# Attention's output projection in three passes by token halves, its division on GpSimd, and the next gated layer begun on the first half

## What is computed

```python
def step(carry, inp):                       # linear attention, 16 heads of 128
    state, z = carry
    q_s, k_s, v_s = inp
    ...
    den = jnp.einsum('bhe,bhe->bh', q_s, z)[..., None] + EPS
    return ((state, z), num / den)
...
return out @ Wo.T                           # 2048 -> 256
...
x = x + s * g                               # g = silu(mixture-of-experts layer of xn)
xn = _layernorm(x, axis=-1)
s = _L1_attn_ref(xn, ...)                   # state-space layer, needs xn
g = _silu(_L1_ffn_ref(xn, ...))             # gated layer: down(silu(gate) * up), hidden width 704
x = x + s * g
```

## Time and profile before

| | before |
|---|---|
| median of 3 runs | 1776.23 us (1775.18 to 1776.37) |
| the profiled execution, its own time | 1777.31 us |
| its span (first to last instruction) | 1775.5 us |
| PE busy | 1648.1 us (93% of the span) |
| DVE / ACT / POOL busy | 1156.9 / 760.2 / 664.7 us (65% / 43% / 37%) |
| mean granted clock of TensorE | 0.971 |

### The profile page before, as it was taken

How to read it: one execution, slowest core, us unless ns; L and a number is a source line. 1 busy time by engine, 2 the same in 40 slices (tenths; PEclk the granted TensorE clock), 3 DMA queues, 4 the chain that set the end, 5 groups by cost and what they waited for, 6 DMA issues and landing times.

```text
span 1775.5 us, 29643 instructions
## 1 busy us (share of the span) xinstructions
PE 1648.1 (93%) x11068; PEld 1366.1 (77%) x11068; DVE 1156.9 (65%) x2041; ACT 760.2 (43%) x1393; POOL 664.7 (37%) x500
## 2 busy tenths in 40 slices
PE   5997899898999999999869978998989999999988
PEld 3886677787878888887848857777978888888878
DVE  4333788663767788876743347886536677777767
ACT  4343445433434444444543334553334444444445
POOL 1453444200324444453514534441003244444535
PEclk9998999999999999999979989999999999999999
DMA  2333000000253344341023320000002533443410
GB/s 77 101 108 118 18 37 1 0 1 10 72 166 121 120 137 137 120 134 34 26 68 107 117 94 19 36 1 1 1 10 71 166 120 122 139 134 119 138 29 25
DMA packets 60061, 135.68 MB, mean 76 GB/s; under 512 B 8128, under 2 KB 12736, under 8 KB 59408
## 3 DMA queue, kind: packets, MB, share of 16 engines
q1 hardware_dynamic: 59920, 133.79, 23.6%
HBM read 130.81 MB, written 2.95 MB: 75 GB/s over the span
## 4 chain that ended last, share of the span: by engine, by line
PE 67%; DVE 11%; POOL 7%; issue 6%; ACT 5%; DMA 2%; SPq 0%; POOLq 0%; DVEq 0%; ACTq 0%
PE ps L553 31%; PE ps L610 6%; PE ps L872 4%; PE ps L896 4%; PE ps L649 4%; PE ps L834 3%; PE ps L589 3%; POOL silu_g L451 3%; PE ps L908 3%; POOL rb L469 2%; POOL fw_lo L436 2%; PE ps L883 2%; PE ps L751 2%; PE ps L752 2%; DVE hid L1347 2%
## 5 line engine op out<-in xcount | busy, mean ns | idle before, releaser
L553 PE MATMUL ps<-xnT_hi,w_in_hi 128*128 128x512 f32 x512 | 222.8, 435 | 0.0
L553 PE MATMUL ps<-xnT_lo,w_in_hi 128*128 128x512 f32 x512 | 203.6, 398 | 0.0
L553 PE MATMUL ps<-xnT_hi,w_in_lo 128*128 128x512 f32 x512 | 203.1, 397 | 0.0
L469 POOL TENSOR_TENSOR rb<-ra,rb 128x512 f32<-128x512 f32 x80 | 117.6, 1470 | 205.0 <-DVE rb L1537 205.0
L427 POOL TENSOR_TENSOR w_in_lo<-w_raw,w_in_hi 128x1024 fp32r<-128x1024 f32 x32 | 85.0, 2658 | 224.3 <-ACT w_in_hi L954 224.3
L1347 DVE TENSOR_TENSOR hid<-ps,silu_g 128x512 f32<-128x512 f32 (+1 forms) x80 | 55.1, 689 | 162.4 <-POOL silu_g L451 106.3
L1659 DVE TENSOR_TENSOR_SCAN lmat<-dec,ident 128x512 f32<-128x512 f32 x128 | 160.6, 1295 | 0.0
L516 POOL TENSOR_TENSOR yt<-yg,sz 128x512 f32<-128x512 f32 x64 | 83.5, 1305 | 155.4 <-ACT sz L1265 148.4
L553 PE MATMUL ps<-xnT_hi,fw_hi 128*128 128x512 f32 x312 | 126.7, 406 | 10.5 <-DVE fw_lo L1365 4.3
L436 POOL TENSOR_TENSOR fw_lo<-fw_raw,fw_hi 128x512 fp32r<-128x512 f32 (+1 forms) x56 | 62.7, 1121 | 185.3 <-ACT fw_hi L984 134.6
L1681 DVE TENSOR_TENSOR mt<-ps,lmat 128x512 f32<-128x512 f32 x128 | 82.5, 686 | 66.1 <-PE ps L872 66.1
(11 more groups left out here) (194 smaller groups left out, 4397.8 us busy)
## 6 DMA issues: line engine op xcount, KB each, us to landing
dec<-dec_dram SPq DMA_DIRECT2D x64, 512.0 KB, 4.0
w_raw<-in_w_in SPq DMA_DIRECT2D x32, 512.0 KB, 4.7
wdec<-dec_dram SPq DMA_DIRECT2D x128, 128.0 KB, 3.9
pdec<-dec_dram SPq DMA_DIRECT2D x128, 128.0 KB, 3.7
fw_raw<-in_fw SPq DMA_DIRECT2D x40, 384.0 KB, 3.1
w_raw<-in_w_qkv SPq DMA_DIRECT2D x8, 768.0 KB, 4.2
comb<-comb_dram SPq DMA_DIRECT2D x8, 512.0 KB, 3.7
w_out<-in_w_o SPq DMA_DIRECT2D x2, 2048.0 KB, 10.8
```

Of the source, the lines that this page charges most:

```text
L469: nc.gpsimd.tensor_tensor(rb[:, k], ra[:, k], rb[:, k], ALU.add).then_inc(a_rot.sem, 1)
L553: mm = nc.tensor.matmul(out, left(l, k), right(r, k), start=(j == 0), stop=(j == len(steps) - 1))
```

## The change

**The projection** now goes by token halves and tiles of the inner width: 2 halves x 16 tiles = 32 units `n`. Per unit PE makes 4 transposes (straight from `y`, into bank `n % 3`) and 12 matmuls of 256 columns in three fp32r passes, which gather in banks 4 and 5 for half 0 and 6 and 7 for half 1. `w_out` is split to `wa_hi`, `wa_lo` on the way (in units 0 to 15), and the transposed `y` to `yTs_hi`, `yTs_lo` (3 slots).

**The division** moves from DVE to POOL: 32 instructions per batch of 128 x (4 x 128), in place in `y`. The first six (`EARLY_NORM`) stand ahead of the end of phase 2. DVE only makes `1/den`, in two pairs of small instructions.

**The barrier** behind the projection is gone. The layernorm of chunks 0 to 3 runs in the second half's units, and PE starts `gate_up` (0,0) on the first token half right after the last projection matmul. The gated layer's first four units go in the order (0,0), (1,0), (0,1), (1,1) (`FFN1_ORDER`), and the decay's matmuls go to banks 6 and 7, one half at a time.

The core of the diff (`-` lines of removed helpers that stand in the kernel above are cut):

```diff
+EARLY_NORM = 6
...
+FFN1_ORDER = [(0, 0), (1, 0), (0, 1), (1, 1)] + [(k, hf) for k in range(2, NF1) for hf in range(2)]
...
+                def normalised(n):
+
+                    hf, t = n // NT - 2 * b, n % NT
+                    pool.wait_ge(rin_step, 4 * b + (2 if t < (KVH - 1) * REP else 4))
+                    part = y[:, 4 * hf:4 * hf + 4, t * P:(t + 1) * P]
+                    nc.gpsimd.tensor_tensor(part, part, rin[:, 4 * hf:4 * hf + 4, t:t + 1].broadcast_to([P, 4, P]), ALU.mult).then_inc(o_yn.sem, 1)
+                for n in range(2 * b * NT, 2 * b * NT + EARLY_NORM):
+                    normalised(n)
                 end_phase(pool, b, 2)
-                end_phase(pool, b, 3)
+                for n in range(2 * b * NT + EARLY_NORM, 2 * (b + 1) * NT):
+                    normalised(n)
...
+                def turn(n):
+                    hf, t = n // NT - 2 * b, n % NT
+                    pe.wait_ge(o_yn.sem, o_yn.done(n))
+                    pe.wait_ge(o_yl.sem, o_yl.done(n - 3))
+                    for j in range(4):
+                        mm = nc.tensor.transpose(ps[:, n % 3, j * P:(j + 1) * P], y[:, 4 * hf + j, t * P:(t + 1) * P], ident4[:, 0:P])
+                    mm.then_inc(o_tr.sem, 1)
+
+                def project(n):
+                    hf, t = n // NT - 2 * b, n % NT
+                    if hf == 0:
+                        pe.wait_ge(o_wh.sem, o_wh.done(b * NT + t))
+                        pe.wait_ge(o_wl.sem, o_wl.done(b * NT + t))
+                    pe.wait_ge(o_yh.sem, o_yh.done(n))
+                    pe.wait_ge(o_yl.sem, o_yl.done(n))
+                    for j in range(4):
+                        for x, (l, r) in enumerate(SPLITS):
+                            mm = nc.tensor.matmul(ps[:, 4 + 2 * hf + j // 2, (j % 2) * DM:(j % 2 + 1) * DM], yTs[l][:, n % YSLOTS, j * P:(j + 1) * P],
+                                                  wa[r][:, t, :], start=(t == 0 and x == 0 and j % 2 == 0), stop=(t == NT - 1 and x == 2),
+                                                  skip_group_check=True)
                     mm.then_inc(o_mm.sem, 1)
...
+                turn(n0 + 1)
+                for n in range(n0, n0 + 2 * NT):
+                    if n + 2 < n0 + 2 * NT:
+                        turn(n + 2)
+                    project(n)
+                    t = n - n0 - NT
+                    if t >= 0 and t % 3 == 2 and t // 3 < 4:
+                        ln_transposes((b * 2 + 1) * NC + t // 3, t // 3 % 2, 3)
 
             def out_proj1(b):
 
...
+                def decay(hf):
+
+                    for c in range(2 * (1 - hf), 4):
+                        pe.wait_ge(o_sg.sem, o_sg.done(b * NC + 4 + c))
+                    pe.wait_ge(ln_hi.sem, ln_hi.done((b * 2 + 1) * NC + 4 * hf + 3))
+                    pe.wait_ge(ln_lo.sem, ln_lo.done((b * 2 + 1) * NC + 4 * hf + 3))
+                    return three_passes(ps[:, 6 + hf, :], lambda l, k: w_dec[l][:, k, :],
+                                        lambda r, k: xnT[r][:, k, hf * HALF:(hf + 1) * HALF])
...
+                pe.wait_ge(o_yl.sem, o_yl.done(2 * (b + 1) * NT - 1))
+                pe.wait_ge(ln_hi.sem, ln_hi.done((b * 2 + 1) * NC + 3))
+                pe.wait_ge(ln_lo.sem, ln_lo.done((b * 2 + 1) * NC + 3))
                 gate_up(b, NF0, 0)
-                pe.wait_ge(s_dec.sem, s_dec.done(b))
-                gate_up(b, NF0, 1)
-                for u in range(2 * NF1):
-                    k = (u + 2) // 2
-                    if u + 2 < 2 * NF1:
-                        gate_up(b, NF0 + k, u % 2, together=(k == NF1 - 1))
-                    down(b, NF0 + u // 2, u % 2, u < 2, u >= 2 * NF1 - 2, rows=(64 if u >= 2 * NF1 - 2 else P))
+                ln_turned(4)
+                decay(0)
+                ln_turned(5)
+                gate_up(b, NF0 + 1, 0)
+                ln_turned(6)
+                ln_turned(7)
+                decay(1).then_inc(s_loga.sem, 1)
+                gate_up(b, *ffn1(2))
+                for x in range(2 * NF1):
+                    if 0 < x < 2 * NF1 - 2:
+                        gate_up(b, *ffn1(x + 2), together=(FFN1_ORDER[x + 2][0] == NF1 - 1))
+                    k, hf = FFN1_ORDER[x]
+                    if x == 2:
+                        pe.wait_ge(s_dec.sem, s_dec.done(b))
+                    if x == 0:
+                        for c in range(4):
+                            pe.wait_ge(o_sg.sem, o_sg.done(b * NC + c))
+                    down(b, NF0 + k, hf, k == 0, k == NF1 - 1, rows=(64 if k == NF1 - 1 else P))
 
 
...
+                def w_hi_of(t):
+                    if t == 0:
+                        act.wait_ge(w_out_in, 16 * (2 * b + 1))
+                    nc.scalar.activation(wa[0][:, t, :], w_out[:, t, :], ACT.Copy).then_inc(o_wh.sem, 1)
+
+                def y_hi(n):
+                    act.wait_ge(o_tr.sem, o_tr.done(n))
+                    act.wait_ge(o_mm.sem, o_mm.done(n - YSLOTS))
+                    nc.scalar.activation(yTs[0][:, n % YSLOTS, :], ps[:, n % 3, :], ACT.Copy).then_inc(o_yh.sem, 1)
+
+                n0, n1 = 2 * b * NT, (b * 2 + 1) * NC
+                for n in range(n0, n0 + 2 * NT):
+                    t = n - n0 - NT
+                    if t < 0:
+                        w_hi_of(n - n0)
+                    y_hi(n)
+                    if 0 <= t < 12 and t % 3 == 0:
+                        ln_std_of(n1 + t // 3, t // 3 % 2)
+                    if 3 <= t < 15 and t % 3 == 0:
+                        ln_hi_of(n1 + t // 3 - 1, t // 3 - 1, (t // 3 - 1) % 2, 3)
+                    if t in (1, 2, 4, 5):
+                        weights_hi1(b, *{1: (0, 0), 2: (0, 1), 4: (1, 0), 5: (1, 1)}[t])
+                for c in range(4, NC + 2):
+                    if c == 7:
+                        silu(b, NF0, 0, s_gu[:, 0, 0:1])
+                    if c < NC:
+                        ln_std_of(n1 + c, c % 2)
+                    if c >= 6:
...
+                def decay():
+                    act.wait_ge(s_loga.sem, s_loga.done(b))
+                    nc.scalar.activation(dec_e[:].rearrange("p (h c) -> p h c", h=2), ps[0:SH, 6:8, :], ACT.Exp).then_inc(own_act, 1)
+                    act.wait_ge(own_act, b + 1)
+                    nc.scalar.activation(dec_t[:], dec_e[:], ACT.Exp, scale=-1.0).then_inc(s_dec.sem, 1)
...
+                for x, (k, hf) in enumerate(FFN1_ORDER):
                     rows = 64 if k == NF1 - 1 else P
-                    silu(b, NF0 + k, hf, s_gu[0:rows, k, 0:1], rows)
+                    if x == 2:
+                        decay()
+                    if x > 0:
+                        silu(b, NF0 + k, hf, s_gu[0:rows, k, 0:1], rows)
                     hidden_hi(b, NF0 + k, hf, s_gu[0:rows, k, 1:2], rows)
-                    if k + 1 < NF1:
-                        weights_hi1(b, k + 1, hf)
+                    if x > 1 and x // 2 + 1 < NF1:
+                        weights_hi1(b, x // 2 + 1, x % 2)
...
+                def w_low(t):
+                    dve.wait_ge(o_wh.sem, o_wh.done(b * NT + t))
+                    nc.vector.tensor_tensor(wa[1][:, t, :], w_out[:, t, :], wa[0][:, t, :], ALU.subtract).then_inc(o_wl.sem, 1)
+
+                def y_low(n):
+                    dve.wait_ge(o_yh.sem, o_yh.done(n))
+                    dve.wait_ge(o_mm.sem, o_mm.done(n - YSLOTS))
+                    nc.vector.tensor_tensor(yTs[1][:, n % YSLOTS, :], ps[:, n % 3, :], yTs[0][:, n % YSLOTS, :], ALU.subtract).then_inc(o_yl.sem, 1)
+
...
+                    nc.vector.tensor_tensor(chunk(x_res, c), sg[:, c % 2], chunk(x_res, c), ALU.add).then_inc(o_res.sem, 1)
+                    dve.wait_ge(o_res.sem, o_res.done(n))
+                    ln_stats(n1 + c, c, c % 2, n1 + c - 2)
+                    ln_variance(n1 + c, c % 2, n1 + c - 2)
...
+                for n in range(n0, n0 + 2 * NT):
+                    t = n - n0 - NT
+                    if t < 0:
+                        w_low(n - n0)
+                    y_low(n)
+                    if 0 <= t < 12 and t % 3 == 0:
+                        add_gated(t // 3)
+                    if 0 <= t < 12 and t % 3 == 1:
+                        normal(t // 3)
+                    if 3 <= t < 15 and t % 3 == 0:
+                        ln_low(n1 + t // 3 - 1, t // 3 - 1, (t // 3 - 1) % 2, 3)
+                    if t in (2, 5, 8, 11):
+                        weights_lo1(b, *{2: (0, 0), 5: (0, 1), 8: (1, 0), 11: (1, 1)}[t])
+                add_gated(4)
+                add_gated(5)
+                normal(4)
+                add_gated(6)
+                normal(5)
+                ln_low(n1 + 4, 4, 0, 3)
+                hidden(b, NF0, 0, f_silu, unit(b, NF0, 0))
+                add_gated(7)
+                normal(6)
+                ln_low(n1 + 5, 5, 1, 3)
+                normal(7)
+                ln_low(n1 + 6, 6, 0, 3)
+                ln_low(n1 + 7, 7, 1, 3)
```

(6 more changed lines are left out.)

203 lines of the change are left out of this document (63 added, 140 removed).

## The result

The changed kernel takes 1781.24 us (median of 20 runs, 1779.3 to 1784.56). The kernel before takes 1776.9 us in the 20 runs beside it (1770.42 to 1783.23). The ratio is 1.0026, with a 95% interval of 1.0015 to 1.0038. So the change costs 4.3 us by the medians, and 2.7 to 6.8 us by the interval. The forecast was 1782. Its sign, slower, came true as well, though the change is little more than the 0.2% that the prediction took as the least that can be told.

A forecast was written before the change was run, and what follows sets the result against it. It took PE to bound the projection and a chain through all engines the part behind. Per batch, 11.6 us lost behind less 8.8 gained gives +2.8, for both +5.6: 1782 us, own range 1778 to 1787, overall 1770 to 1792.

The forecast's parts named there:

- Projection, work and start: In the projection: matmuls at 0.12 us each give PE back 9.2 us; the first projection starts at 356.9.
- Projection, new waits: In the projection's second half: PE waits 2.1 us at unit 17 and 0.6 at unit 20, 2.7 in all.
- the meeting with DVE: In the projection: POOL and DVE hinder each other, slowing POOL to 1.7 us per tile, until about 396.
- The rival in which POOL sets the pace: In the projection: POOL's form takes 1.8 us, so the projection ends some 8 us later per batch; 1798, chance 0.10.
- The lock itself: On POOL and DVE: a DVE instruction on two SBUF operands waits for POOL's to end, 1.60 us instead of 0.69.
- Behind the projection, idle: From the projection's end to the last down: PE idles 19.5 us instead of 8.3.
- The queue walk: Behind the projection: following the engines' lists gives waits of 1.35, 5.0, 1.4, 7.0, 2.9, 0.7 and 1.2 us.
- one fall of the clock as before: Behind the projection: PE's clock falls once per batch, as in the old kernel, costing 1.6 us.
- two as a rival with 0.17: Behind the projection: the clock falls twice per batch, 2 x 1.6 us more, 1785; chance 0.17.
- The second batch counts the same: In the second batch: same instructions, so the same +2.8 us as the first, +5.6 for both.
- The table loads: On ACT behind the projection: each load costs 1.28 us, without the added 1.38 us drain, which would add 2.8.
- The faster rival: Before gate_up (1,1): ACT runs both exponentials under PE's work, so the 7.0 us wait does not arise; 1768, chance 0.15.

The follow-up runs named there:

- e1_bank: The changed kernel, but each decay part waits only until its own bank has been read; 1779.12 us, ratio 1.0015 to the kernel before.
- e3_exp: The changed kernel with silu (0,1) ahead of hidT_hi (1,0) and both exponentials later on ACT, hid (0,1) ahead of hidT_lo (1,0) on DVE; 1769.13 us.

## Why the prediction was right

The kind of the change was foreseen: the projection gives time back, the waits behind it take more. But the forecast of 1782 for 1781.24 is better than its working, and that it hit within 1 us is luck. Three steps were off, by 1.7 us per batch, by 2.4 and, in the second batch alone, by 2.1, the first and the last against the second.

- **Projection, work and start.** Right: matmuls of 0.12 us, a first projection at 356.93 for 356.9, the six divisions in attention's shadow.
- **Projection, new waits.** Too high: I had 2.1 us at unit 17 and 0.6 at unit 20, and the trace has 0.97 and none. The mis-sized term is POOL's instruction. I had taken 1.27 us and 1.7 with the meeting with DVE; it takes less, in the group of all 32 and in the six ahead of the phase's end:

```profile
L514 POOL TENSOR_TENSOR y<-y,rin 128x512 f32<-128x512 f32 x32 | 35.3, 1138 | 10.7 <-DVE rin L1684 6.2 <-ACTq L349 4.5
```

```profile
344.22 6.07 POOL L514 TENSOR_TENSOR y<-y,rin 128x512 f32<-128x512 f32 x6 [6.25 <-DVE rin L1684]
```

  That is 1.14 and 1.01 us. DVE was busy for 2.4 of these 6.07 us, with six instructions that each read one operand from `ps`. The meeting itself is there, and DVE pays most of it: the 16 subtractions `wa_lo` (L1433, 256 columns), for which I had 0.42 us alone, take 0.51 to 1.26 us and 0.84 on average, one of them

```profile
364.06 1.26 DVE L1433 TENSOR_TENSOR wa_lo<-w_out,wa_hi 128x256 fp32r<-128x256 f32 x1
```

  while POOL makes its other 26 in 29.22 us, 1.12 each instead of 1.01. So the step that failed is that the meeting slows POOL to 1.7. POOL is done with its 32 by 384, and no longer runs on to 396 into the second half, where I had it hold up DVE. The projection ends 63.90 us behind attention instead of 74.42, 10.5 us earlier for the 8.8 of the sum. The rival in which POOL sets the pace (1.8 us) is out.
- **The lock itself** is there. `hidT_lo` on DVE takes 0.75 us alone and 2.04 when POOL has begun a suffix product before it; the second of these rows stands ahead of the weights that `gate_up` (3,0) waits for, 3.41 us (I had 2.9).

```profile
441.03 0.75 DVE L1408 SCALAR_TENSOR_TENSOR hidT_lo<-hid,s_gu,hidT_hi 128x512 fp32r<-128x512 f32 x1 [4.04 <-ACT hidT_hi L1028]
...
462.23 2.04 DVE L1408 SCALAR_TENSOR_TENSOR hidT_lo<-hid,s_gu,hidT_hi 128x512 fp32r<-128x512 f32 x1 [0.79 <-ACT hidT_hi L1028]
```

- **Behind the projection, idle.** The queue walk held: 0.82 for 1.35, 4.73 for 5.0, 1.14 for 1.4, 7.01 for 7.0, 3.41 for 2.9, 1.16 for 1.2; 18.27 for 19.5 in sum, where the second small wait, of 0.7, did not come. e1_bank shows what the walk had left out, `gate_up` (1,0)'s wait for `hid` (0,0), which lay behind a longer one.
- **The clock.** The step "one fall of the clock as before" failed. There are three, after the waits of 4.73, 7.01 and 3.41 us, and they cost about 1.5 + 1.7 + 2.7 = 5.9 us (2.90 for six decay matmuls that take 1.40; 4.49 and 5.46 for 2.79), where I had 1.6. I had two as a rival with 0.17. The part behind the projection is 14.0 us longer instead of 11.6. That the clock falls once per batch was not even true of the kernel before: in its second batch the rows below show it slow in the decay, in a `gate_up` and in the last `down`.
- **"The second batch counts the same"** failed too, and it is what brought the sum back. The chain of the second batch, of the kernel before and then of the changed one:

```profile
1315.65 5.47 PE ps L553 x12
...
1329.83 4.33 PE ps L553 x12
...
1375.38 2.74 PE ps L589 x12
```

```profile
1313.24 2.90 PE ps L581 x6
...
1334.47 4.57 PE ps L581 x12
...
1352.33 5.46 PE ps L581 x12
...
1380.60 1.66 PE ps L616 x12
```

  The kernel before pays for the clock there in the decay (5.47) and in a `gate_up` (4.33), 2.3 us more than in its first batch, of the 2.9 by which the stages differ in this one execution. Past the stage its last `down` is slow as well (2.74 against 1.67). The changed kernel's second stage is only 0.8 longer than its first. So the change costs 3.5 us in the first batch and 1.4 in the second, for the 2.8 and 2.8 of the sum, and the slow `down` of the kernel before takes 1.1 off the 4.9 again: the spans differ by 4.1, the medians by 4.3. I had the second fact in the earlier trace rows (5.3 us at 0.50) and used it for a rival only.
- **The table loads** go by the row: in the chain above `hidT_hi` ends at 441.00, the load starts at 441.02 and lasts 1.28, and the exponential starts at 442.31. The Trainium skill, "ScalarE: Activation LUTs", section "What ACT_TABLE_LOAD costs", adds a drain of 1.38 us to each switch; this trace does not show it.

The faster rival (exponentials hidden) did not happen in this kernel, but e3_exp shows that one edit of the order hides them, and that it is worth 12 us.

## What to carry to other kernels

When work is made to start earlier, walk each engine's list from there to the next point that all need, and ask of each instruction that waits what stands behind it: here two exponentials ahead of a silu cost 6 us per batch, more than half of what the new projection gave. Split such a change in two: the new projection alone was worth 16 us, and the new order behind it hid that. Price a wait of PE of several microseconds with the slow clock behind it, here 1.5 to 2.7 us each, and do so for each batch of the kernel before as well. And expect that a wait taken away uncovers the next, here 2.48 us for one of 4.73.
